# Routed pieces of 256 rows, two to a step, and moved by SyncE

## The reference

```
scores = softmax(xf @ gate_w.T)                     # xf: 4096 x 128
_, idx = top_k(scores + gate_b, 2)                  # two experts of eight for each token
h  = silu((xf @ w1[e] + b1[e]) * (xf @ w3[e] + b3[e]))   # 176 hidden units
oe = h @ w2[e] + b2[e]
y  = sum over the two experts of scores[e] * oe
z  = the same with the shared expert's weights
return y + z
```

## Time and profile before

| | before |
|---|---|
| median of 3 runs | 2947.47 us |
| all runs | 2938.24 to 2947.93 us |
| profiled execution, its own time | 2940.1 us |
| its span | 2938.8 us |
| PE busy | 2498.9 us, 85% |
| DVE busy | 2084.1 us, 71% |
| ACT busy | 1787.1 us, 61% |
| POOL busy | 1173.5 us, 40% |
| granted clock of PE, mean | 0.923 |

### The profile page before, as it was taken

The page is one execution under the profiler, slowest core; times in us unless marked ns, Lnnn a source line. Parts: engine busy times, 40 slices in busy tenths (PEclk is TensorE's granted clock), DMA queues, the critical chain, the costliest instruction groups (busy, mean ns, idle before and its releaser), DMA issues.

```text
span 2938.8 us, 67833 instructions
## 1 busy us (share of the span) xinstructions
PE 2498.9 (85%) x25429; PEld 1973.6 (67%) x25429; DVE 2084.1 (71%) x7719; ACT 1787.1 (61%) x3496; POOL 1173.5 (40%) x1616
## 2 busy tenths in 40 slices
PE   7799998769699668559589999999999998895886
PEld 4467775446477546336389899999988996563555
DVE  6667766873377844754388888888888888446877
ACT  5444445434255334336379999999999995563553
POOL 4200002570374657565642332322244433556413
PEclk9799999879899889679799999999999998997997
DMA  9910000014210123325200000000010100441001
GB/s 233 281 43 3 3 3 1 11 47 145 90 35 10 37 92 122 101 78 166 91 15 18 17 21 14 21 14 14 14 34 25 35 23 9 124 156 31 25 7 30
DMA packets 126503, 164.59 MB, mean 56 GB/s; under 512 B 15457, under 2 KB 94946, under 8 KB 126178
## 3 DMA queue, kind: packets, MB, share of 16 engines
q1 hardware_dynamic: 98242, 86.58, 10.7%
q0 software_dynamic: 27936, 73.66, 8.3%
HBM read 85.18 MB, written 75.01 MB: 55 GB/s over the span
## 4 chain that ended last, share of the span: by engine, by line
PE 39%; DVE 13%; POOL 4%; issue 3%; ACT 1%; DMA 1%; DVEq 0%; POOLq 0%; ACTq 0%
PE banks L3627 6%; PE banks L3612 6%; PE banks L3557 3%; PE banks L3574 2%; PE banks L3593 2%; PE banks L3566 2%; PE banks L3550 2%; PE banks L3592 1%; PE banks L3304 1%; PE banks L3315 1%; PE banks L3317 1%; PE banks L3305 1%; PE banks L3306 1%; POOL results L1511 1%; POOL bins L3269 1%
## 5 line engine op out<-in xcount | busy, mean ns | idle before, releaser
L3627 PE MATMUL banks<-layer,shared_floats 128*128 128x128 f32 x2048 | 292.0, 275 | 0.0
L3728 POOL TENSOR_SCALAR shared_floats<-shared_floats 128x2 f32<-128x2 f32 x256 | 57.7, 225 | 582.6 <-DVE shared_floats L3719 579.0
L3627 PEld LDWEIGHTS banks<-layer,shared_floats 128*128 128x128 f32 x2048 | 258.8, 192 | 0.0
L3612 PE MATMUL banks<-shared_floats,layer 128*128 128x256 f32 x1024 | 243.8, 381 | 0.0
L4017 ACT ACTIVATE shared_floats<-banks,layer 128x256 f32<-128x256 f32 x512 | 210.3, 471 | 50.8 <-PE banks L3612 50.8
L3612 PEld LDWEIGHTS banks<-shared_floats,layer 128*128 128x128 f32 x1024 | 185.9, 192 | 20.2
L3730 POOL TENSOR_TENSOR shared_floats<-shared_floats,neg_half 128x2 f32<-128x2 f32 x256 | 183.7, 717 | 21.3
L3740 DVE TENSOR_SCALAR shared_floats<-banks,shared_floats 128x128 f32<-128x128 f32 x512 | 185.5, 404 | 7.2 <-POOL shared_floats L3730 7.2
L2213 DVE TENSOR_REDUCE shared_floats<-banks 128x2 f32<-128x512 f32 (+3 forms) x256 | 110.7, 484 | 91.0 <-PE banks L2077 89.5
L2318 ACT ACTIVATE shared_floats<-banks 128x480 f32<-128x480 f32 (+1 forms) x192 | 83.6, 488 | 139.7 <-PE banks L2084 139.7
L256 PE MATMUL banks<-ident,xn 128*128 128x128 f32 x320 | 59.8, 318 | 127.4 <-issue 76.2
(11 more groups left out here) (445 smaller groups left out, 7926.9 us busy)
## 6 DMA issues: line engine op xcount, KB each, us to landing
bins<-zero SPq DMA_DIRECT2D x1, 18176.0 KB, 70.0
layer<-in_dram_layers SPq DMA_DIRECT2D x16, 902.0 KB, 4.6
bins<-layer SPq DMA_DIRECT2D x16, 650.0 KB, 13.0
shared_floats<-bins SPq DMA_DIRECT2D x32, 325.0 KB, 3.8
expert_weights<-in_dram_experts SPq DMA_DIRECT2D x32, 312.0 KB, 3.1
outs<-shared_floats SPq DMA_DIRECT2D x16, 320.0 KB, 3.3
results<-zero SPq DMA_DIRECT2D x1, 4096.0 KB, 16.1
bins<-xn,f_bin_row POOLq DMA_INDIRECT x256, 2.3
```

The source lines that it names most:

```text
L3612: m = T.matmul(k.bank[5 + half][:, part], w["w1"][:, tile(n)], h1[:, :], start=True, stop=True)
L3627: m = T.matmul(to, hidden[:, n * S + t * P:n * S + (t + 1) * P], w["w2"][:, tile(n)], start=False, stop=(n == NF - 1), skip_group_check=True)
```

## The change

The piece shrinks to 256 rows, and a step works on two pieces, which can belong to different experts: columns 0 to 255 with the first expert's weights, 256 to 511 with the second's. There are 40 pieces (32 + 8) in 20 steps (`PAIRS`) instead of 23. A step needs two sets of weights; the second ring of four lies in the buffers `e_rows` of the sixteen-expert stage. The wide products, the lift and the multiplication are issued for each half; transposes, narrow products, SiLU and copies are not changed in number for a step.

`pieces_gpsimd` goes, and `pieces_sync` comes: SP loads each piece's first row number from partition 0 of the tables into a register (`value_load`) and issues a direct DMA at that address; rows first, then weights, each with a semaphore of its own. The tables' entries are now one row number for a piece instead of 128. `routed_sync` becomes `ffn2_sync`, which also loads the first two layers of the encoder before the pieces of run 0; `att2_sync` keeps the others.

```diff
-PIECE = CH
-PIECES = 2 * N // PIECE + E2 - 1
-ALL_PIECES = E2 * N // PIECE + E2 - 1
+PIECE = CH // 2
+PAIRS = (2 * N // PIECE + E2) // 2
+PIECES = 2 * PAIRS
+LIMITS = N // PIECE
+ALL_PIECES = E2 * N // PIECE + PIECES - 2 * N // PIECE
...
-def routed_sync(k, s):
-
-    if s.before == "ffn1" and s.kind == "ffn2":
+def ffn2_sync(k, s):
+
+    if s.before == "ffn1":
         load_results(k, s)
+    if s.run == 0:
+        for run in range(2):
+            load_layer(k, run)
+    pieces_sync(k, s)
...
-    v.count(V.tensor_tensor(by_expert(square[:, :], E2), carry.unsqueeze(2).broadcast_to([P, E2, E2]),
-                            limits.unsqueeze(1).broadcast_to([P, E2, E2]), ALU.is_gt))
+    v.count(V.tensor_tensor(by_expert(over[:, :], LIMITS), carry.unsqueeze(2).broadcast_to([P, E2, LIMITS]),
+                            limits.unsqueeze(1).broadcast_to([P, E2, LIMITS]), ALU.is_gt))
...
-    return {"w": k.sb(f"expert_weights{m % W_RING}", [P, BIASED_WIDTH]), "rows": k.sb(f"g_rows{m % W_RING}", [P, PIECE]),
+    return {"w": [k.sb(f"expert_weights{m % W_RING}", [P, BIASED_WIDTH]), k.sb(f"e_rows{m % W_RING}", [P, BT * ROW])[:, 0:BIASED_WIDTH]],
+            "rows": k.sb(f"g_rows{m % W_RING}", [P, CH]),
...
-        T.matmul(up[:, :], w[:, tile(1)], rowsT[:, :], start=True, stop=True)
-        T.matmul(gate[:, :], w[:, tile(0)], rowsT[:, :], start=True, stop=True).then_inc(k.sem("g_gate_up"), 1)
-        T.matmul(tails[0:TAILS, :], w[:, 2 * P:DOWN], rowsT[:, :], start=True, stop=True).then_inc(k.sem("g_gate_up"), 1)
+        T.wait_ge(k.sem(f"e_weights_in{m % W_RING}"), EXPERTS_FETCHED + 32 * (m // W_RING + 1))
+        for to, columns in ((up, tile(1)), (gate, tile(0)), (tails[0:TAILS, :], slice(2 * P, DOWN))):
+            for h in range(2):
+                ins = T.matmul(to[:, half(h)], w[h][:, columns], rowsT[:, half(h)], start=True, stop=True, skip_group_check=True)
+            if to is not up:
+                ins.then_inc(k.sem("g_gate_up"), 1)
...
-            V.scalar_tensor_tensor(out=hidden[part][0:rows, :], in0=gates[0:rows, :], scalar=w[0:rows, bias:bias + 1],
-                                   in1=up, op0=ALU.add, op1=ALU.mult).then_inc(k.sem("g_product"), 1)
+            for h in range(2):
+                ins = V.scalar_tensor_tensor(out=hidden[part][0:rows, half(h)], in0=gates[0:rows, half(h)],
+                                             scalar=w[h][0:rows, bias:bias + 1], in1=up[:, half(h)], op0=ALU.add, op1=ALU.mult)
+            ins.then_inc(k.sem("g_product"), 1)
...
-        A.activation(b["hidden"][0][:, :], up[:, :], ACT.Identity,
-                     bias=w[:, GATED_WIDTH + 1:GATED_WIDTH + 2]).then_inc(k.sem("g_identity"), 1)
+        for h in range(2):
+            ins = A.activation(b["hidden"][0][:, half(h)], up[:, half(h)], ACT.Identity,
+                               bias=w[h][:, GATED_WIDTH + 1:GATED_WIDTH + 2])
+        ins.then_inc(k.sem("g_identity"), 1)
...
-def pieces_gpsimd(k, s):
...
+def pieces_sync(k, s):
+
+    SP, m0 = k.nc.sync, s.run * PAIRS
+    by_twos = lambda rows: rows.rearrange("(p two) d -> p (two d)", two=PIECE // P)
+
+    def rows_at(m, h):
+        at = 2 * (m - m0) + h
+        return SP.value_load(piece_index(k, "rows")[0:1, at:at + 1], min_val=0, max_val=(ALL_PIECES - 1) * PIECE)
+
+    def fetch_weights(m):
+        if m - m0 >= W_RING:
+            SP.wait_ge(k.sem("g_down"), m - W_RING + 1)
+        for h in range(2):
+            at = 2 * (m - m0) + h
+            first = SP.value_load(piece_index(k, "weights")[0:1, at:at + 1], min_val=0, max_val=E2 * P)
+            SP.dma_start(piece_buffers(k, m)["w"][h][:, :], k.d["dram_experts8"][bass.ds(first, P), :]
+                         ).then_inc(k.sem(f"e_weights_in{m % W_RING}"), 16)
+
+    def fetch_rows(m):
+        if m - m0 >= W_RING:
+            SP.wait_ge(k.sem("g_turned"), m - W_RING + 1)
+        for h in range(2):
+            SP.dma_start(piece_buffers(k, m)["rows"][:, half(h)], by_twos(k.bins8[bass.ds(rows_at(m, h), PIECE), :])
+                         ).then_inc(k.sem(f"e_rows_in{m % W_RING}"), 16)
+
+    def store(m):
+        SP.wait_ge(k.sem("g_out"), m + 1)
+        for h in range(2):
+            SP.dma_start(by_twos(k.bins8[bass.ds(rows_at(m, h), PIECE), :]), piece_buffers(k, m)["out"][:, half(h)]
+                         ).then_inc(k.sem(f"results_moved{m % 2}"), 16)
+
+    SP.wait_ge(k.sem("g_index"), s.run + 1)
+    for slot in range(XN_RING):
+        SP.wait_ge(k.sem(f"f1_sent{slot}"), 16 * K1 * ((s.c0 + NC - 1 - slot) // XN_RING + 1))
+    for m in range(m0, m0 + 3):
+        fetch_rows(m)
+        fetch_weights(m)
+    for m in range(m0, m0 + PAIRS):
+        if m + 3 < m0 + PAIRS:
+            fetch_rows(m + 3)
+            fetch_weights(m + 3)
+        if m > m0:
+            store(m - 1)
+    store(m0 + PAIRS - 1)
```

More of the change, by code:

```diff
@@ L971, with wait_pair_stored @@
 OUTS_STORED = 16 * E1 // 2
+RESULTS_LOADED = OUTS_STORED + 32 * NC // 2
+EXPERTS_FETCHED = 16 * 2 * E1 // W_RING
+def wait_pair_stored(k, engine, m):
+    engine.wait_ge(k.sem(f"results_moved{m % 2}"), RESULTS_LOADED + 32 * (m // 2 + 1))
 def wait_out_stored(k, engine, m):
@@ L3041, in place_last @@
         choose_piece_rows(k, s, i)
-    of_pieces = [k.sb(f"g_hidden1_{n}", [P, PIECE])[:, :] for n in range(2)]
+    of_pieces = [k.sb(f"g_hidden1_{n}", [P, CH])[:, :] for n in range(2)]
     if A:
@@ L3126, in choose_pieces @@
     V, v = k.nc.vector, k.v
-    table = k.sb("g_table", [P, PIECES + E2 + E2 * E2])
-    ids, limits, upto = table[:, 0:PIECES], table[:, PIECES:PIECES + E2], table[:, PIECES + E2:PIECES + E2 + E2 * E2]
+    table = k.sb("g_table", [P, PIECES + LIMITS + E2 * E2])
+    ids, limits, upto = (table[:, begin:begin + width] for begin, width in
+                         ((0, PIECES), (PIECES, LIMITS), (PIECES + LIMITS, E2 * E2)))
+    over = k.sb("g_over", [P, E2 * LIMITS])
     square, needed, ends = k.sb("g_square", [P, E2 * E2]), k.sb("g_needed", [P, E2]), k.sb("g_ends", [P, E2])
@@ L3273, in piece_buffers, with half @@
 def piece_buffers(k, m):
-    return {"w": k.sb(f"expert_weights{m % W_RING}", [P, BIASED_WIDTH]), "rows": k.sb(f"g_rows{m % W_RING}", [P, PIECE]),
-            "rowsT": k.sb(f"g_rowsT{m % 2}", [P, PIECE]), "up_tail": k.sb(f"g_up_tail{m % 2}", [P, PIECE]),
-            "hidden": [k.sb(f"g_hidden{part}_{m % 2}", [P, PIECE]) for part in range(2)],
-            "out": k.sb(f"g_out{m % 2}", [P, PIECE])}
+    return {"w": [k.sb(f"expert_weights{m % W_RING}", [P, BIASED_WIDTH]), k.sb(f"e_rows{m % W_RING}", [P, BT * ROW])[:, 0:BIASED_WIDTH]],
+            "rows": k.sb(f"g_rows{m % W_RING}", [P, CH]),
+            "rowsT": k.sb(f"g_rowsT{m % 2}", [P, CH]), "up_tail": k.sb(f"g_up_tail{m % 2}", [P, CH]),
+            "hidden": [k.sb(f"g_hidden{part}_{m % 2}", [P, CH]) for part in range(2)],
+            "out": k.sb(f"g_out{m % 2}", [P, CH])}
+def half(h):
+    return slice(h * PIECE, (h + 1) * PIECE)
 def piece_banks(k, m):
@@ L3323, in pieces_tensor @@
     turn(m0)
-    for m in range(m0, m0 + PIECES):
+    for m in range(m0, m0 + PAIRS):
         widen(m)
-        if m + 1 < m0 + PIECES:
+        if m + 1 < m0 + PAIRS:
             turn(m + 1)
@@ L3329, in pieces_tensor @@
             narrow(m - 1)
-    narrow(m0 + PIECES - 1)
+    narrow(m0 + PAIRS - 1)
     behind = range(shared_before_pieces(s), NC)
@@ L3341, in pieces_vector @@
 def pieces_vector(k, s):
-    V, m0 = k.nc.vector, s.run * PIECES
+    V, m0 = k.nc.vector, s.run * PAIRS
     def multiply(m):
@@ L3380, in pieces_scalar @@
 def pieces_scalar(k, s):
-    A, m0 = k.nc.scalar, s.run * PIECES
+    A, m0 = k.nc.scalar, s.run * PAIRS
     def copy_rows(m):
@@ L3421, in pieces_scalar @@
         shared8_silu(k, s, i)
-def pieces_gpsimd(k, s):
[L3428 to L3442, removed]
-    def store(m):
[L3445 to L3450, removed]
```

63 lines of the change are left out of this document (30 added, 33 removed).

## The result

The changed kernel takes 2976.3 us (median), the kernel before 2946.5 us on the same chip: a ratio of 1.0094, 95% interval 1.0076 to 1.0112. It is slower by some 28 to 30 us, where a gain of 27 us was forecast. The profiled execution took 2968.8 us with a span of 2967.5, against 2940.1 and 2938.8 before.

The account below looks back on a forecast made before the run. PE was taken to bound both stretches. Terms -28.8 + 0.8 - 1.3 + 0.8 + 1.8 = -26.7 us took 2940.1 to 2913.4; the forecast was put at 2917, likeliest case 2903 to 2928, whole range 2903 to 3014.

Parts of the forecast that it names:

- V + D: SP's time per loaded address (V) plus its direct DMA (D, taken as 0.42 us), six of each a step.
- rivals 2 and 3: SP's serial chain sets both stretches' ends from V + D = 0.86, costing 220 us per us; chances 0.14 and 0.33.
- V = 0.20: On SP, a loaded address with bounds checks and address arithmetic was taken to cost 0.20 us, between 0 and 0.97.
- rival 3: SP bounds both stretches by far, from V + D = 1.05 on; 3030 us at 0.97 us a load; chance 0.33.
- 0.46: Chance given to the forecast case, PE still the bound, a loaded address costing 0 to 0.40 us, 2903 to 2928 us.
- Steps removed: In each stretch of experts' pieces, 23 steps of 4.80 us become 20: 28.8 us less in all.
- The step on PE: Wide products split into halves of 256 columns and an added weights wait: 0.02 us a step, 0.8 us in all.
- ACT and DVE: Lift and multiplication in halves on these engines: cost nothing, hidden by PE; otherwise 0.4 us a step.
- Start: First stretch's beginning: SP orders rows before weights, so rows land earlier, 1.3 us gained; nothing in the second.
- End: Each stretch's end: last results stored by two DMAs behind two loads, +0.9 us, twice, 1.8 us.
- choosing: Choosing pieces with larger tables: +0.8 us, hidden by the sends in the first stretch, paid in the second.
- Rival 1: In the piece steps the DMA engines fill: at 218 GB/s a step takes 5.35 us, total 2935 us; chance 0.06.

Follow-up runs that it names:

- experiment 6: The changed kernel with the 240 addresses loaded without lower and upper bounds: 2923.2 us, ratio 0.9922 to the kernel before.
- experiment 3: The changed kernel with a piece's row address kept in SP's register from fetch to store, four loads a step: 2943.8 us, ratio 0.9989 to the kernel before.
- experiment 2: The changed kernel with each of the 240 addresses loaded twice, the first value unused: 3099.8 us, ratio 1.0533 to the kernel before.
- experiment 1: The changed kernel with constant addresses, no loads, same transfers, pieces not following the routing: 2913.8 us, ratio 0.9899 to the kernel before.
- (9): The changed kernel with row addresses kept from fetch to store and all addresses loaded without bounds, SP alone: 2913.8 us, ratio 0.9894 to the kernel before.
- experiment 4: The changed kernel with POOL loading the stores' addresses and issuing the stores: 2916.3 us, ratio 0.9911 to the kernel before; repeated, 2916.6 us, 0.9893.
- 5: The kernel before with wide products, lift and multiplication issued in halves of 256 columns, its gathers kept: 2951.3 us, ratio 1.0011 to the kernel before.

## Why the prediction was wrong

Its own formula for SP, 2913 us plus 220 us for each us that V + D is above 0.86, is held against the runs here. The step is the mean distance of the stores in SP's queue in the first stretch, while fetches still stand between them (1332.45 to 1434.72 in the changed kernel, 15 steps); that takes in the slower steps, in which one load or one DMA took longer.

| kernel | steps averaged | SP's step, us | V + D = step / 6 | formula, us | profiled execution, us |
|---|---|---|---|---|---|
| without bounds (6) | 15 | 5.30 | 0.883 | 2918 | 2923.3 |
| kept addresses (3) | 15 | 5.86 | 0.977 | 2939 | 2946.4 |
| changed kernel | 15 | 6.82 | 1.136 | 2974 | 2968.8 |
| loaded twice (2) | 9 | 10.14 | 1.690 | 3096 | 3093.0 |

It holds within 8 us over a range of 170 us, and where SP's step is below PE's the times are nearly flat: 2911.2 (1), 2910.9 (9), 2916.8 (4). The mechanism, its place and its price were those of rivals 2 and 3. **The step that failed is the value of one term, "I take V = 0.20".** It measures 0.69 us (V + D = 1.11 less D = 0.42). With 0.69 the text's own working gives 2913 + 220 x 0.25 = 2968, and the profiled execution took 2968.8. That the two agree within 1 us is in part luck: with the mean step of 6.82 us the formula gives 2974, and the start came out 2 us worse than forecast. The price itself is borne out by a difference as well: with the loads the two stretches take 136.6 + 131.6 us, with constants 107.8 + 103.9, 56.5 us less, where 220 x 0.25 is 55.

The choice went by kind: "the last is nearest in kind (a few values, no descriptors)". DVE's 0.09 us in the earlier trace rows is an instruction of another engine, and one instruction. On SP the load alone takes 0.27 us, register work and gaps follow it, and nearly nothing overlaps: a second load whose value nobody uses adds 0.56 us (experiment 2). The argument for rival 3 said so ("a round trip [...] in front of every DMA, in one serial queue"), and the difference of 0.59 us between an indirect and a direct DMA was 0.10 off. By the text's own formula the sign turned at V = 0.56 (2913 + 220 x 0.12 = 2940), not far above the middle between the ends of 0 and 0.97, and the 0.59 lay above it. A cost of which only bounds were known decided the sign, and no row of its own kind bore out the 0.46 that stood on V under 0.40. The range of that case, 2903 to 2928, was also wider than the terms that it names: V from 0 to 0.40, the start and the base together give some 2911 to 2923.

The Trainium skill's page "DMA: Bandwidth & Descriptors", in "Latency and other measured facts", has a floor of about 600 ns for such a load. The instruction itself takes 0.27 us in this trace, so the row does not agree with the page; what a loaded address costs in all, 0.69 us, is nearer to the page's figure than to the 0.20 that I took.

Point by point:
- **Steps removed**, 28.8 us: right. 40 copies out, and a step of 4.82 us where SP is not late.
- **The step on PE**, 0.02 us: right (4.82 and 4.81 us, experiments 4 and 5).
- **ACT and DVE**, nothing: right while PE bounds. DVE's half took 0.48, not 0.43 us, and it did not matter: experiment 1 has PE at 99%.
- **D = 0.42**: right within 0.05. Without a load between, a DMA starts 0.44 us after the one before it in experiment 3 (1371.47 to 1371.91), and the second of two stores 0.47 us after the first. With 0.44 for D, V is 0.67.
- **Start**, 1.3 us gained: wrong. Rows landed as forecast (SP's first load at 1309.16, transposes at 1313.48, 4.3 us; forecast 4.4), but the first wide product waited for weights ordered behind them and came 3.87 us after the transposes, against 1.76 before. From the landing of the last sent rows to the first product it is 1317.35 - 1309.07 = 8.3 us, before 1314.33 - 1306.73 = 7.6: 0.7 us lost. The working put the weights 1.24 us behind the rows; they were issued 2.56 us behind (1311.28 to 1313.84) and took 3.4 to land.
- **End**, +0.9 us a stretch, and **choosing**, +0.8: not measured one by one. With SP's loads gone (experiment 1) the two stretches together are 27.6 us shorter, against a forecast of 26.7 for the whole sum, which had V = 0.20 in it.
- **Rival 1**: did not come. The DMA engines reach 226 GB/s at a share of 0.73 in experiment 4, with PE at its own pace.
- **What would show it** named the observation that decided: "above 1.05, rival 3, with PE waiting for the weights' or rows' DMA in each step". Of rival 3, the size (3030 us) was too high, as V was 0.69 and not 0.97, and the clock did not fall: 0.99 and 1.00 at 82% busy.

## What to carry to other kernels

When an edit moves address work onto one queue, count the addresses and multiply by what a load costs in that queue with all that follows it, not by one instruction: 6 x 1.11 us did not fit into a step of 4.80 us, although six DMAs alone (2.5 us) did. Where the unknown cost decides the sign, say at which value it does and let the chances follow how much of its bounds lies on either side. And before giving up such a change, look for what is paid twice: keeping an address in a register together with dropping its bounds, or giving the stores' loads to a queue that was idle, turned a loss of 0.9% into a gain of 1.1%.

## What the runs showed of the hardware

- An address loaded on SP with bounds costs 0.69 us ahead of its DMA: 0.27 us for the load, 0.28 for the bounds (experiment 6), 0.14 for offset arithmetic and gaps. A second load whose value nobody uses costs 0.56 us (experiment 2), so nearly nothing of it overlaps.
- A load right behind two DMAs that were issued 0.47 us apart took 0.64 us in the step shown, against 0.27 elsewhere (experiment 3). Why was not tried.
- In the window where PE was 82% busy (the changed kernel) it was granted a clock of 0.99; in the window where it was 68% busy (experiment 2) it was granted 0.87, a mean over both levels of the clock.
- POOL issues a direct DMA of 128 KB in 0.54 us and loads an address in 0.31 (experiment 4), against SP's 0.35 and 0.27.
